# Adding the output bias of two self attentions by a one-row product on TensorE instead of by GpSimd's adds on the residual

## What is computed

```python
qkv = x @ w_qkv                      # the second: x @ W_qk and x @ W_v
dots = jnp.einsum('bhid,bhjd->bhij', q, k) * scale   # the second adds a bias by distance
attn = jax.nn.softmax(dots, axis=-1)
out = jnp.einsum('bhij,bhjd->bhid', attn, v)
out = out.transpose(0, 2, 1, 3).reshape(b, n, H * hd)
return out @ w_out + b_out           # b_out: 256 values, the same for every token
```

## Time and profile before

| | before |
|---|---|
| median of 3 runs (lowest to highest) | 1342.28 us (1341.74 to 1342.65) |
| profiled execution, its own time | 1330.97 us |
| its span, first to last instruction | 1329.2 us |
| PE busy | 1192.8 us, 90% |
| DVE busy | 709.3 us, 53% |
| ACT busy | 556.1 us, 42% |
| POOL busy | 383.6 us, 29% |
| mean granted TensorE clock | 0.935 of 2.4 GHz |

### The profile page before, as it was taken

How to read it: one execution, slowest core, us unless ns; L and a number is a source line. 1 busy time by engine, 2 the same in 40 slices (tenths; PEclk the granted TensorE clock), 3 DMA queues, 4 the chain that set the end, 5 groups by cost and what they waited for, 6 DMA issues and landing times. The chain is left out here.

```text
span 1329.2 us, 32322 instructions
## 1 busy us (share of the span) xinstructions
PE 1192.8 (90%) x13863; PEld 1048.1 (79%) x13863; DVE 709.3 (53%) x1127; ACT 556.1 (42%) x907; POOL 383.6 (29%) x339
## 2 busy tenths in 40 slices
PE   4799999999999999999999988796699999278799
PEld 4789889889889899899998977674477778266598
DVE  5555655565565575475475443275564222565732
ACT  4455555555555555555555532214532322111400
POOL 4632332332332342342242210053144000540000
PEclk9899999999999999999999985597989999589989
DMA  6937647647657556566665460190012121414045
GB/s 197 209 85 174 154 102 165 146 116 159 138 132 149 132 140 141 132 145 137 141 149 124 104 128 1 54 363 2 1 68 87 57 64 48 127 28 191 2 176 194
DMA packets 61732, 161.47 MB, mean 121 GB/s; under 512 B 24904, under 2 KB 38296, under 8 KB 58520
## 3 DMA queue, kind: packets, MB, share of 16 engines
q1 hardware_dynamic: 58904, 154.18, 46.0%
q0 software_dynamic: 1536, 4.20, 0.9%
q10 hardware_dynamic: 1152, 1.05, 0.2%
HBM read 70.56 MB, written 9.44 MB: 60 GB/s over the span
## 5 line engine op out<-in xcount | busy, mean ns | idle before, releaser
L366 ACT ACTIVATE xa_pt<-xa_sc 128x1024 f32<-128x1024 f32 (+1 forms) x224 | 212.4, 962 | 151.2 <-PE xa_sc L558 151.1
L412 DVE TENSOR_REDUCE xa_mx<-xa_sc 128x2 f32<-128x804 f32 x256 | 243.4, 991 | 41.4 <-PE xa_sc L542 41.4
L558 PE MATMUL xa_sc<-xa_queries,xa_keys 104*128 104x128 f32 (+1 forms) x1664 | 232.5, 285 | 2.4 <-DVE xa_queries L427 1.8
L558 PEld LDWEIGHTS xa_sc<-xa_queries,xa_keys 104*128 104x128 f32 (+1 forms) x1664 | 206.6, 196 | 21.0 <-issue 8.4
L479 PE MATMUL xa_pj<-xa_ctx_hi,xa_wk 128*128 128x400 f32 (+1 forms) x512 | 157.0, 349 | 0.9 <-DVE xa_qst L440 0.9
L479 PE MATMUL xa_pj<-xa_wv,xa_ctx_hi 128*128 128x256 f32 (+1 forms) x832 | 155.3, 286 | 0.1
L542 PE MATMUL xa_sc<-xa_keys,xa_queries 96*128 96x402 f32 x512 | 138.0, 373 | 13.0 <-DMA xa_keys<-xa_kst_hi 7.3
L569 PE MATMUL xa_op<-xa_pt,xa_values 128*32 128x64 f32 x6656 | 141.8, 228 | 7.7 <-ACT xa_pt L366 3.3
L295 POOL TENSOR_TENSOR xa_ctx_lo<-xa_raw,xa_ctx_hi 128x1600 fp32r<-128x1600 f32 (+1 forms) x32 | 115.9, 3623 | 78.0 <-DVE xa_ctx_hi L405 75.4
L300 POOL TENSOR_TENSOR xa_kst_lo<-xa_wk,xa_kst_hi 128x400 fp32r<-128x400 f32 x64 | 67.3, 1051 | 227.4 <-ACT xa_kst_hi L345 227.4
L479 PEld LDWEIGHTS xa_pj<-xa_wv,xa_ctx_hi 128*128 128x128 f32 (+1 forms) x832 | 126.2, 185 | 8.0 <-issue 6.5
(11 more groups left out here) (286 smaller groups left out, 1736.7 us busy)
## 6 DMA issues: line engine op xcount, KB each, us to landing
xa_keys<-xa_kst_hi SPq DMA_DIRECT2D x256, 200.2 KB, 6.1
xa_keys<-xa_kst_lo SPq DMA_DIRECT2D x128, 200.2 KB, 5.4
xa_raw<-in_ctxT SPq DMA_DIRECT2D x15, 1601.0 KB, 9.0
gf_w<-in_gf_w SPq DMA_DIRECT2D x16, 1024.0 KB, 7.1
moe_ex<-in_moe_ex SPq DMA_DIRECT2D x8, 1088.0 KB, 15.9
xa_queries<-xa_qst SPq DMA_DIRECT2D x96, 32.0 KB, 3.5
moe_slots_in<-in_moe_zero SPq DMA_DIRECT2D x1, 2944.0 KB, 16.4
moe_xs<-moe_slots_in SPq DMA_DIRECT2D x23, 128.0 KB, 2.2
```

What stands on the lines that cost most here:

```text
L366: nc.scalar.activation(PT[ptslot(step)][0:rows, 0:nt], SC[bank(step)][0:rows, 0:nt], ACT.Exp, scale=float(D0) ** -0.5).then_inc(ex_done, 1)
L412: nc.vector.tensor_reduce(mx[:, u // 2, 2 * (u % 2):2 * (u % 2) + 2], SC[bank(step)][:, :, 0:MXN], AX.X, ALU.max).then_inc(mx_done, 1)
L558: last = mm(SC[bank(step)][0:rows, kk, a * P:(a + 1) * P], KS[:, 2 * a + h, kt * P:kt * P + rows], QS[b % 2][:, 2 * a + h, :], start=True, ...
```

## The change

The eight adds of GpSimd go in both self attentions. Each `project` gets a third product into the same PSUM tile: a row of 128 ones (one contraction row) times the first partition of the bias row, 256 columns. The row of ones is a new tile of one partition, filled once in each attention by a memset of GpSimd. VectorE's `add` no longer waits for `bias_added`, and TensorE waits for the row of ones once, ahead of the first scores. The spread load of the bias row stays.

```diff
@@ self_attention
+        row_of_ones = sb("row_of_ones", [1, P])
@@ project, on the tensor engine
                 for k in range(2):
-                    last = mm(WP[:, 0, 0:D], oT[:, k, :], W["o"][:, k, :], start=k == 0, stop=k == 1)
-                last.then_inc(y_full, 1)
+                    mm(WP[:, 0, 0:D], oT[:, k, :], W["o"][:, k, :], start=k == 0, stop=False)
+                mm(WP[:, 0, 0:D], row_of_ones[:], bias[0:1, :], start=False, stop=True).then_inc(y_full, 1)
@@ before, on the tensor engine
+                pe.wait_ge(row_ready, 1)
                 projected(pe, 2)
                 scores(0, 0)
@@ the gpsimd program
             zeros_and_ones(nc.gpsimd, 0)
+            nc.gpsimd.memset(row_of_ones[:], 1.0).then_inc(row_ready, 1)
 
             pool.wait_ge(ones[0], 2)
             for m, name in enumerate(split_order):
                 pool.wait_ge(w_hi, m + 1)
                 nc.gpsimd.tensor_tensor(WL[name][:], W[name][:], WH[name][:].bitcast(f32), ALU.subtract).then_inc(w_lo, 1)
-            add_bias(nc, pool, X, bias, w_in, loaded, bias_added)
@@ add, on the vector engine
-                dve.wait_ge(bias_added, T)
                 dve.wait_ge(y_full, t + 1)
```

More of the change, by code:

```diff
@@ L665, in add_bias @@
         nc.gpsimd.tensor_tensor(X[:, t], X[:, t], row[:], ALU.add).then_inc(added, 1)
-ATTENTION_SEMS = ("ln_hi", "ln_lo", "w_hi", "w_lo", "pj", "pj_free", "rot", "ones0", "ones1", "bias_added", "km_pool", "km_act", "v_in",
+ATTENTION_SEMS = ("ln_hi", "ln_lo", "w_hi", "w_lo", "pj", "pj_free", "rot", "ones0", "ones1", "row_of_ones", "km_pool", "km_act", "v_in",
                   "s_full", "t_full", "o_full", "ot_full", "y_full", "mx", "sub", "exp", "t_ev", "rcp", "norm", "ot_ev", "y_ev", "stats")
@@ L715, in self_attention @@
         ln_hi, ln_lo, w_hi, w_lo = [sems[n] for n in ("ln_hi", "ln_lo", "w_hi", "w_lo")]
-        pj, pj_free, rot_done, bias_added, stats_done = [sems[n] for n in ("pj", "pj_free", "rot", "bias_added", "stats")]
+        pj, pj_free, rot_done, row_ready, stats_done = [sems[n] for n in ("pj", "pj_free", "rot", "row_of_ones", "stats")]
         ones = [sems[f"ones{e}"] for e in range(2)]
```

## The result

The kernel after takes 1352.61 us, the median of 6 runs (1352.33 to 1355.63), and the kernel before took 1342.1 us in 6 runs beside it (1338.86 to 1343.43). The ratio is 1.0087, with a 95% interval of 1.0072 to 1.0101. By the ratio that is 11.7 us slower, where 7.6 were forecast (the two medians lie 10.5 us apart; the ratio is not taken from them). The profiled execution took 1352.62 us, its span is 1350.8 us, and the mean granted clock fell from 0.935 to 0.928.

What follows compares the result with a forecast made beforehand. The prediction took the second self attention's ring through `project`, with no TensorE slack, as the bound; the first had 0.34 us idle cover. Terms: 2.3 us first plus 5.3 us second, 7.6 us, giving 1349.9 us; range 1345.8 to 1353.5.

Steps and rivals of the forecast that it cites:

- The price of the one-row product, 0.60 us: Each projection: two records and one more change of array shape, with its drain, add 0.60 us on TensorE.
- without a drain: Rival, both attentions: no drain, so 0.43 us a product and 4.8 us in total, 1347.1 us; chance 0.2.
- a nearly free product: The fourth rival, both attentions: 0.03 us a record, 0.5 us in total, 1342.8 us; chance 0.05.
- Seven steps of `sb` at 0.60: Second self attention: seven projections stand in the loop's ring, each adding its full 0.60 us, 4.2 us.
- The last `project` of `sb`, 1.2 us: End of the second self attention: the eighth projection, counted at half clock, adds twice 0.60, 1.2 us.
- 0.1 us back from VectorE: Second self attention: without GpSimd's adds beside it, VectorE's second `lnL` gets 0.1 us shorter, to 1.1 us.
- The steps of `sa`, 2.3 us: First self attention: 0.60 at the first projection, 6 x 0.19 = 1.1 in steps, 0.60 at the last, together 2.3 us.
- Work on GpSimd at nothing: Both attentions: the new memset hides in GpSimd's idle time and costs nothing; uncovered, 0.3 us each.
- The second rival: Behind both attentions and at the first's last projection: half-clock stretches lengthen, 3.6 us more, 1353.5 us; chance 0.12.
- Nothing behind takes it back: Stages behind: the feed-forward's TensorE chain starts when the stage before ends, so none of the 7.6 us is recovered.
- The third rival: Behind both attentions: added records keep the clock up, 4.9 us back, 2.3 in the feed-forward's first group, 1345.0 us; chance 0.03.
- On the median, 1342.28 + 7.6: Whole kernel: the 7.6 us costed on the profiled execution of 1330.97 us, added to the median, 1349.9 us.

Runs made afterwards that it cites:

- experiments 3: Changed kernel with a full 128-row product of 1/128 times the spread bias in place of the one-row product; ratio 1.0007.
- 7: Changed kernel with two one-row products of 0.5 each per projection in place of one; ratio 1.0144.
- experiment 11: Kernel before, adds kept, plus an unread one-row, two-column product of zeros after each projection; ratio 1.0017.
- experiment 2: Kernel before without the output bias in either self attention: no adds, no wait for them, no product; ratio 0.9987.
- experiment 13: The changed kernel run again with no edit; ratio 1.0110.
- experiment 6: The change in the second self attention alone, the first keeping GpSimd's adds; ratio 1.0045 against the kernel before.
- 5: The change in the first self attention alone, the second keeping GpSimd's adds; ratio 1.0070 against the kernel before.
- 4: Changed kernel with the one-row product moved ahead into TensorE's idle time, where it opens the sum in PSUM; ratio 0.9994.
- 9: Kernel with the 128-row product, plus a ScalarE copy of 128 columns in steps of the first self attention; ratio 1.0020.
- r14_drain_longer: Kernel before with the unread two-column one-row product and the added ScalarE copy in the first self attention; ratio 1.0057.
- 16: Kernel before with a ScalarE copy of 512 columns in each step of the first self attention; ratio 1.0030.
- r8_longer_step: Kernel before with a ScalarE copy of 128 columns in all but the last two steps of the first self attention; ratio 1.0018.
- 12: Changed kernel with the product made 128 rows and also moved ahead into TensorE's idle time; ratio 0.9995.
- 10: Changed kernel with 32 contraction rows of 1/32 in place of the one row of ones; ratio 1.0104.

## Why the prediction was right and wrong

- **The price of the one-row product, 0.60 us.** Right: +0.62 in `sb`, +0.64 at the first `project` of `sa`. Its parts hold too: 0.43 for two records at the pitch of 128-row ones (experiments 3 and 7), and 0.2 more for the drain; a change of shape with two records of two columns costs 0.31 (experiment 11). The weight load, for which the prediction had no row, shows in the kernel after: a median of 184 ns for one row and 190 ns for 128. The rivals without a drain and with a nearly free product fall.
- **Seven steps of `sb` at 0.60.** They grew by 0.56 us; the idle time ahead of the add by 0.55, to 0.84 us. The prediction put the removal of VectorE's wait for `bias_added` at nothing; it gives back 0.07 us a step (experiment 2), and 0.62 - 0.07 is the 0.55.
- **The last `project` of `sb`, 1.2 us.** Mis-sized: 1.66 us, since the clock was at half from its first record on. In other executions of the same instructions it was 0.3 to 0.7 us, so the forecast of this term had no firm ground.
- **0.1 us back from VectorE.** Wrong, and small: the second `lnL` took 1.22 us after, not 1.1.
- **The steps of `sa`, 2.3 us.** Right as costed: 0.64, six times 0.22 and 0.55, together 2.5.
- **Work on GpSimd at nothing.** Right. GpSimd's new memset took 0.31 us, and GpSimd then idled 0.90 us for `wh_q`, which was 1.00 in the earlier trace rows:

```profile
1202.41 0.31 POOL L879 MEMSET sb_row_of_ones<- 1x128 f32 x1
1203.62 2.35 POOL L884 TENSOR_TENSOR sb_wl_q<-sb_w_q,sb_wh_q 128x1024 fp32r<-128x1024 f32 x1 [0.90 <-ACT sb_wh_q L1029]
```

- **The step that failed** is the sum for `sa` at a clock taken as unchanged: "6 x 0.19 = 1.1 us" counts six steps at 2.4 GHz. Three of them fell to 1.2 GHz for a while, and lost 4.9 us more, two thirds of what `sa` lost. The second rival had the kind of loss and nearly its size (3.6 us), but placed it behind both attentions and at the last `project`.
- **"Nothing behind takes it back".** Not so in this profile. The third rival (chance 0.03) had the feed-forward's first group give back 2.3 us, and it gave 2.1: 5.91 us in the earlier trace rows, and here, then in experiment 13:

```profile
1291.26 3.81 PE gf_hp L1621 x32
```

```profile
1292.15 5.93 PE gf_hp L1621 x32
```

In the five profiles whose `sb` is that of before, this group takes 5.3 to 5.9 us and the feed-forward 67.1 to 67.7; in eleven of the other thirteen 3.81 us and 65.4 to 65.9; in two with the change in `sb` (experiments 6 and 13) it is as before. So a changed `sb` often, and not always, moves the clock's fall away from the feed-forward. It is one of the prediction's own signs of being wrong: the clock behind a stage changed by microseconds, to the better. The mean over the context swings without such an order (22.1 to 25.8 us over all the profiles), and nothing here ties its 2.1 us less to the change. That the time came out only some 3 to 4 us above the forecast is luck in part: `sa` and `sb` alone lost 13.5 us, and these two stages took 4.3 us off that.
- **"On the median, 1342.28 + 7.6".** The sum could be put on the median. But the gap of 11.3 us between median and profiled execution is as large as what one stage differs by from chip to chip, and I had named the gap without asking which stage might hold it.
- **A slip without effect.** In the fourth rival, ten products at 0.25 us are 2.5 us, not 2.7.

The Trainium skill says (TensorEngine Tiling (Array Packing), Key Properties) that a change of the tiling mode makes TensorE drain; the 0.31 us of experiment 11 agree.

The cause is shown as far as this: the product in this place brings the spells (5, 6), the same product in idle time doesn't (4), a full-array one doesn't even in an equally long step (3, 9), drains with a longer step do (14), and so does a much longer step without either (16). What stays open is why, at 6.01 us and with the same records otherwise, `r14_drain_longer` has spells and `r8_longer_step` has none, and so what in the drains tips it; each verdict on spells rests on one profiled execution of its kernel; only the change itself has two, and before has two (and its `sa` two more, in experiment 6 and, without the adds, in experiment 2). The pairs also cross chips: `r8_longer_step`, `r11_drain_only` and `r14_drain_longer` ran on three, and the change itself never ran on the chip of experiments 3 and 4. Experiments 9 and 12, without spells, and 10, with two, did share one.

## What to carry to other kernels

Where a loop leaves TensorE idle for part of every step, cost a change to it at both clock levels, not only by what it adds to the ring: 0.2 us a step brought 4.9 us in three spells. A one-row product is no cheaper than a full one and changes the array's shape as well; give it all rows (a spread operand over 1/128) and issue it ahead, opening the sum in PSUM, where the engine waits anyway. Here even that gained nothing over GpSimd's adds, which stood in nobody's way. A wait that was met long ago isn't free in a ring: it cost 0.07 us a step. Before two profiles are compared, cut them by stages and run the kernel before again on more chips: the largest difference here belonged to neither kernel.

## What the runs showed that I had not expected

- TensorE's granted clock fell to 0.72 over a 6 us window in the middle of a loop in which TensorE waited 1.16 us a step for its keys, and rose again within the step; the same wait, 1.15 us, stands in every step of the kernel before.
- The same kernel takes 10 us less on one chip of four: in the experts' stage ScalarE's longest wait is 13.1 to 14.7 us there and 24.3 to 24.5 us on the others. Where it comes from wasn't tried.
- The first group of the feed-forward took 5.3 to 5.9 us behind the `sb` of before, five times of five, and 3.81 us behind most others.
- A product of one row and two columns still costs 0.31 us, drain and records together, against 0.43 us for a full-array one of 256 columns; and 1 row costs what 32 do.
